# Layer 2 attention: key projections two and two, banks drained ahead of the copy of the inverses, value products from the third step of a round

## The reference, cut to what matters

```python
def _L2_xattn_ref(x, context, mask, Wq, Wkv, Wout, b_out):
    q = x @ Wq.T
    k, v = jnp.split(context @ Wkv.T, 2, axis=-1)
    # q, k, v are split into 16 heads of 64
    sim = jnp.einsum('bhid,bhjd->bhij', q, k) * DIM_HEAD ** (-0.5)
    sim = jnp.where(mask[:, None, None, :], sim, max_neg)
    attn = jax.nn.softmax(sim, axis=-1)
    out = jnp.einsum('bhij,bhjd->bhid', attn, v)
    return out.transpose(0, 2, 1, 3).reshape(B, Nq, HEADS * DIM_HEAD) @ Wout.T + b_out
...
x = x + _L2_xattn_ref(_layernorm(x, axis=-1), ctx_1024, ...)
```

## Time and profile before

| | us |
|---|---|
| median of three timed runs | 1757.13 (1757.09 to 1757.54) |
| profiled execution, its own time | 1760.41 |
| span of its trace, first to last instruction | 1758.5 |
| around the span | 1.9 |
| the stage `wide_attention`, about | 524 (485.5 to 1009.5 in the span) |
| mean granted TensorE clock, whole span | 0.926 |

### The profile page before, as it was taken

One profiled execution on the slowest core, in us unless ns is written; L12 is line 12 of the kernel. 1 busy time (PEld: TensorE's weight loads), 2 busy tenths in 40 slices (PEclk: granted clock), 3 DMA queues, 4 the chain that ended last, 5 costly groups with the idle time before them and its releaser, 6 DMA issues. The chain is left out here.

```text
span 1758.5 us, 44254 instructions
## 1 busy us (share of the span) xinstructions
PE 1535.7 (87%) x16764; PEld 804.3 (46%) x16764; DVE 1303.6 (74%) x3513; ACT 1032.9 (59%) x2227; POOL 569.5 (32%) x618
## 2 busy tenths in 40 slices
PE   5886999997669999999999899979799896999976
PEld 3532344433424444444554556655466652333333
DVE  5636778885878777677777789956899666799847
ACT  2331666665846555556555389854689631777764
POOL 0306656521010000000000289915799303342210
PEclk9895999998869999999999899999999985899997
DMA  5124333301010000000000000010100002322100
GB/s 167 34 31 134 76 80 67 66 14 49 1 38 3 8 2 9 8 3 9 28 3 3 8 1 1 0 40 9 48 1 0 1 14 74 55 43 50 30 2 24
DMA packets 60284, 54.21 MB, mean 31 GB/s; under 512 B 9610, under 2 KB 52798, under 8 KB 59974
## 3 DMA queue, kind: packets, MB, share of 16 engines
q1 hardware_dynamic: 59238, 51.32, 12.1%
q10 hardware_dynamic: 864, 0.39, 0.1%
HBM read 30.59 MB, written 1.05 MB: 18 GB/s over the span
## 5 line engine op out<-in xcount | busy, mean ns | idle before, releaser
L1926 ACT ACTIVATE probs_l2x<-probs_l2x,nmax_l2x 128x512 f32<-128x512 f32 x256 | 182.8, 715 | 193.5 <-DVE nmax_l2x L1797 193.5
L1797 DVE CUSTOM_DVE_ANT_0 probs_l2x<-s_ps_l2x,mask_b_l2x 128x512 f32<-128x512 f32 x256 | 166.6, 689 | 120.5 <-PE s_ps_l2x L2007 120.1
L1072 DVE CUSTOM_DVE_ANT_0 junk_l1x<-s_ps_l1x,mask_b_l1x 128x512 f32<-128x512 f32 x256 | 166.3, 687 | 50.3 <-PE s_ps_l1x L1273 46.0
L1075 DVE TENSOR_REDUCE nmax_l3x<-s_ps_l3x 128x1 f32<-128x512 f32 x256 | 163.7, 683 | 33.6 <-PE s_ps_l3x L1273 31.9
L1134 ACT ACTIVATE pT_l1x<-st_ps_l1x 128x1024 f32<-128x1024 f32 x128 | 131.2, 1025 | 79.9 <-PE st_ps_l1x L1258 79.5
L1809 DVE STREAM_TRANSPOSE pT_l2x<-probs_l2x 128x512 f32<-128x512 f32 x256 | 166.4, 688 | 0.0
L2007 PE MATMUL s_ps_l2x<-kT_l2x_first,q_l2x 64*32 64x512 f32 x2048 | 147.5, 634 | 11.3 <-DVE nmax_l2x L1797 10.5
L2023 PE MATMUL pv_ps_l2x<-pT_l2x,v_l2x_first 32*64 32x256 f32 x4096 | 137.7, 385 | 2.6 <-issue 2.6
L1740 POOL TENSOR_TENSOR spread_l2x<-inv_l2x,consts 128x512 f32<-128x512 f32 x16 | 17.6, 1101 | 324.5 <-DVE inv_l2x L1816 324.5
L2618 POOL TENSOR_TENSOR rn_l2a_first<-ssc_l2a_first,consts 128x16 f32<-128x16 f32 x28 | 109.1, 3897 | 20.2 <-DVE ssc_l2a_first L2645 20.0
L2788 ACT ACTIVATE probs_l2a<-minus_s_l2a,nmax_l2a 128x128 f32<-128x128 f32 (+1 forms) x256 | 106.1, 424 | 9.5 <-DVE nmax_l2a L2693 9.5
(11 more groups left out here) (531 smaller groups left out, 3574.9 us busy)
## 6 DMA issues: line engine op xcount, KB each, us to landing
mask_i_l1x<-in_mask SPq DMA_DIRECT2D x8, 512.0 KB, 4.2
maskT_i_l1x<-in_mask_t SPq DMA_DIRECT2D x8, 512.0 KB, 4.9
kT_l1x_first<-parts_l1x_first SPq DMA_DIRECT2D x60, 64.0 KB
kT_l3x_first<-parts_l3x_first SPq DMA_DIRECT2D x60, 64.0 KB
q_l1x<-parts_l1x_first SPq DMA_DIRECT2D x90, 32.0 KB
q_l3x<-parts_l3x_first SPq DMA_DIRECT2D x90, 32.0 KB
ctxT_l0x<-in_ctxT SPq DMA_DIRECT2D x9, 256.0 KB, 3.1
rows_l0x<-in_ctx SPq DMA_DIRECT2D x9, 256.0 KB, 4.2
```

The costliest lines, as they stand in the source:

```text
L1072: dve.tensor_tensor_reduce(out=junk[w][:], in0=s_ps[w][:], in1=mask_b[b % 2][:, j, :], scale=-1.0, scalar=3e38, op0=ALU.add, op1=ALU.min, ...
L1075: dve.tensor_reduce(to, s_ps[w][:], AX.X, ALU.max, negate=True).then_inc(m.s_drained[w].sem, 1)
L1797: dve.tensor_tensor_reduce(out=probs[n % 4][:], in0=s_ps[w][:], in1=mask_b[b % 2][:], scale=-1.0, scalar=3e38, op0=ALU.add, op1=ALU.min, a ...
L1926: act.activation(probs[n % 4][:], probs[n % 4][:], ACT.Exp, bias=nmax[:, b % 2, n:n + 1], scale=-1.0, accum_out=sums[:, r, w, qb:qb + 1]). ...
```

## The change

Four tables and one order are edited:
- The keys of both tables move from three and one to two and two in the first two steps of a round.
- One query projection of the next batch moves from step 11 to 12, and the second output projection of the batch before from step 12 to 11.
- The value products begin one step later: 3, 3, 3, 3, 2, 2 blocks in steps 2 to 7 of a round in place of 3, 3, 2, 2, 2, 2, 2 in steps 1 to 7.
- On ACT the drains of the step's jobs come before `copy_inv`, not behind it.

```diff
-    this_batch = {0: [(K, 4), (K, 5), (K, 6)], 1: [(K, 7)], 2: [(Q, 2)], 3: [(Q, 3)], 4: [(V, 0)], 5: [(V, 1)], 6: [(V, 2)], 7: [(V, 3)],
+    this_batch = {0: [(K, 4), (K, 5)], 1: [(K, 6), (K, 7)], 2: [(Q, 2)], 3: [(Q, 3)], 4: [(V, 0)], 5: [(V, 1)], 6: [(V, 2)], 7: [(V, 3)],
                   14: [(V, 4), (V, 5)], 15: [(V, 6), (V, 7)]}
-    next_batch = {7: [(XT, 0)], 8: [(K, 0), (K, 1), (K, 2)], 9: [(K, 3)], 11: [(Q, 0)], 13: [(Q, 1)]}
-    last_batch = {10: [(OUT, 0)], 12: [(OUT, 1)]}
+    next_batch = {7: [(XT, 0)], 8: [(K, 0), (K, 1)], 9: [(K, 2), (K, 3)], 12: [(Q, 0)], 13: [(Q, 1)]}
+    last_batch = {10: [(OUT, 0)], 11: [(OUT, 1)]}
...
-    blocks_of = {1: range(0, 3), 2: range(3, 6), 3: range(6, 8), 4: range(8, 10), 5: range(10, 12), 6: range(12, 14), 7: range(14, 16)}
+    blocks_of = {2: range(0, 3), 3: range(3, 6), 4: range(6, 9), 5: range(9, 12), 6: range(12, 14), 7: range(14, 16)}
...
                         if ahead(b, s)[0] < B:
                             exponentials(*ahead(b, s))
+                        for job in steps[b, s]:
+                            drain(job)
                         if s % QB == 0 and n >= 2:
                             copy_inv(n - 2)
-                        for job in steps[b, s]:
-                            drain(job)
```

## The result

The changed kernel takes 1774.14 us (median of 4 runs, 1772.38 to 1774.6) against 1757.3 of the kernel before (4 runs, 1757.09 to 1757.54): ratio 1.0096, 95% interval 1.0081 to 1.0111. It is 1.0% slower, as forecast. Its profiled execution took 1774.27, with a span of 1772.4 at a mean granted clock of 0.918.

The account below looks back on a forecast made before the run. PE was taken to set the pace, pausing 1.82 us for a bank at round starts. Schedule +4.0 and clock +8.7 gave +12.7 on 1757.1: 1769.8 us, range 1759 to 1778.

Parts of the forecast that it names:

- The held maxima: Second scores' maxima wait behind DVE's product, which needs the later copy; PE pauses 2.11 and 0.40, each round 0.22 longer.
- the walk through a round: One profiled round stepped through from its first scores, placing drains, copy, product, reciprocal, maxima and third scores after the change.
- The clock: PE's clock would fall behind the new pauses in 10 of 13 rounds, 1.5 us each, against four before: +8.7 us.
- round 0: Nearest row with so little PE work: only scores, waiting for DVE, with the clock at 0.50 from 494.5 to 504.5.
- Round 1: Without copy or product nothing holds the maxima; its bank wait of 0.69 goes: -0.35 us, between -0.9 and 0.
- The end: Last round: later copy holds the maxima, a bank wait of 0.40, three blocks left: +1.5 us, 0 if hidden.
- The total: Schedule +4.0 and clock +8.7 make +12.7 us; 1773.1 us profiled, 1769.8 us as median.
- the gap between before's profiled execution and its median: The median of the timed runs was taken as 3.3 us below the profiled execution, for the changed kernel too.
- The pause only moves: Rival: the clock falls as often as before, so only the schedule's +4.0 counts: 1761.1 us; chance 0.17.
- the scores keep the clock up: Rival: scores between the two pauses prevent falls, the four old ones go: -2.3 us, 1754.8; chance 0.10.
- DVE isn't held: Rival: maxima go once scores are done, both pauses vanish: -36 us with the four falls, about 1721; chance 0.03.
- 0.03 of slack of the third key: The third key projection's bank was to be free at 740.08, its turn at 740.11: no wait, 0.03 us to spare.

Follow-up runs that it names:

- e4: Changed kernel with the product of outputs and inverses, and the inversion of the sums, one step later on DVE, behind the maxima: 1731.18 us.
- e8: e4 with the product moved between the maxima and the transposes of the second step, the inversion still behind both: 1726.14 us.
- e1: Changed kernel with the copy of the inverses back ahead of the drains on ACT, tables as changed: 1741.58 us.
- e3: Changed kernel with the value products back in the steps they had before, from the second step of a round: 1741.06 us.
- e7: Changed kernel with ACT's order and the value products put back as before, so only the tables of projections are changed: 1734.8 us.
- e5: Changed kernel with the fourth and eighth key projections done three times over, to the same result, filling PE's pause: 1757.61 us.
- e6: Kernel before with the second and sixth key projections done twice, half filling its pause of 1.8 us: 1747.9 us against 1760.38.
- e2: Kernel before with only ACT's order changed, drains ahead of the copy of the inverses: 1751.95 us.
- e9: Kernel before with only the value products moved, to steps three to eight of a round: 1764.68 us (10 runs), 0.35% slower.
- e10: Kernel before with only the second output projection a step earlier and the first query projection a step later: 1761.99 us (12 runs).

## Why the prediction was right

**The held maxima: right.** Every place of the walk through a round is met within 0.07: copy 4.25 (4.27 predicted), product 5.30 (5.30), reciprocal 6.44 (6.44), maxima 6.60 (6.60), third scores 7.90 (7.97). The pauses are 1.96 and 0.23 to 0.33 (2.11 and 0.40 predicted), and clean rounds last 29.4 and 32.8 (29.5 and 32.8 predicted). e4 and e8, which take the product from ahead of the maxima, remove the big pause; e1 and e3, which undo one edit each, do too. A clean pair of rounds is 0.37 longer than before's, 0.19 a round (0.22 predicted), 2.4 over the 13. The idle needs both edits: on top of the tables alone (e7), ACT's order adds 0.10 a round, the moved blocks 0.43, both 1.40 (halves of the differences of clean pairs).

**The clock: right in its sum, off in its parts.** I took 10 falls of 1.5; there were 12, of about 1.28 each. The 1.28 is (417.53 - 402.14) / 12, with the same stretch of e5, which has the same score starts and no falls. 15.4 measured, 15.0 predicted: the direction was reasoned, the closeness is luck, since one part was too low and the other too high. The count had a weak basis too. I leaned on round 0 as a row with as little work as the 1.0 in 3.5 us of the new round start, but that row has PE busy for 7.13 of 10 us. What PE must leave undone for the clock to fall was not found out.

Rounds 2 to 14 grew by 11.31: 2.41 by the schedule and 15.39 by twelve falls, less the 6.49 of before's four (406.22 less 399.73 in e6). 2.9 + 8.7 = 11.6 was predicted. The Trainium skill (TensorE: Matmul & The Clock Gate, HAM oscillation — how this bites in real kernels) would have no fall behind pauses this short. The trace contradicts it in 12 of 13 rounds, and e5 and e6 take the falls away by filling about 1.7 and 0.9 us of the pause.

**Round 1: right.** -0.28 for rounds 0 and 1, -0.35 predicted.

**The end: the term that was mis-sized.** +1.5 predicted for the last round and what follows, +3.99 measured, of which +3.01 lies in the last round. The pause is there as walked through, 2.02 and 0.42, but the clock falls behind it, and my sum had no fall in the last round.

```profile
969.86 1.09 PE L2007 MATMUL s_ps_l2x<-kT_l2x_first,q_l2x 64*32 64x512 f32 x16 [2.02 <-DVE nmax_l2x L1797]
971.37 3.53 PE L1993 MATMUL ring_l2x<-wo_l2x,o_l2x 128*128 128x128 f32 x16 [0.42 <-ACT v_l2x_first L1912]
```

The 16 matmuls of the output projection take 3.53 there and 2.05 at 977.98. That is 1.5, and the other 1.5 is what was predicted for the schedule. The +0.98 behind the last scores is within what the same code does in other traces (779.55 to 783.63). A second spell at 1.2 GHz at 998, which before's trace doesn't have, is not of this change: all twelve traces but before's and e7's have one that starts 8 to 10 us behind the last scores, those with the old key tables (e2, e6, e9, e10) among them.

**The total.** +12.7 predicted and +13.9 measured, span to span; +14.04 within the stage. The forecast of 1769.8 is 4.3 low; 3.3 of that is one choice: I took the gap between before's profiled execution and its median as fixed and carried it over. The changed kernel's profiled execution is at its median, and later medians of before were 1758.5 to 1760.4. Where in the program that gap lay no trace shows, as there is one trace of each kernel.

**The rivals.** "The pause only moves" and "the scores keep the clock up" are ruled out by the 12 falls. "DVE isn't held" came true only where the product was moved: e4 and e8, 1731 and 1726, where I had put about 1721. The 0.03 of slack of the third key held.

## What to carry to other kernels

When work is moved out of a step, look for what that step waits for on the other engines: here three blocks of value products can cover the time that a DVE product takes from the maxima (e3), and two edits that cost 0.10 and 0.43 us a round one by one cost 1.40 together. On an engine that works in order, put the instruction that releases the bottleneck (the maxima) ahead of one that waits for a late copy, not behind it; that alone turned +1.0% into -2.0% (e8). And price a pause of PE with the clock that may fall behind it: the idle was about as long as before (25.5 and 2.5 against 23.7), and more falls were most of the loss (8.9 of the 11.31 in rounds 2 to 14, and half of the 3.01 in the last).

## What was not expected of the hardware

- How often the clock falls differs between traces with the same pauses of 1.82 and the same clean rounds: four falls in before's, six in e10's. Single runs of before lay between 1753.7 and 1761.8; this spread is as large as the effects of e2, e9 and e10. It goes with the granted clock of the whole execution: 0.930 in the fastest of the 23 runs beside e8 to e10 (1753.72) and 0.926 in the slowest (1760.66); in e10's twelve 0.933 (1751.25) and 0.925 (1765.38). Whether these are falls in this stage or elsewhere in the program isn't shown.
- Splitting a pause was enough here: one of 1.82 was followed by falls in 4 to 7 of 13 rounds (before, e10, e9), about the same idle as 0.91 and 0.83 with a key projection, scores and another projection between (e2, one trace) in none, at equal length of the round.
- The code ahead of the stage is the same everywhere, yet the stage's first scores came at 491.96 (before), 490.84 (after) and 486.47 (e9). A difference of a few us between two traces says nothing until the stretch in question is compared.
